# Gate bias of a two-layer graph network: VectorE adds it while moving the gate's product out of PSUM, in place of a matmul with rows of ones

## Reference

```python
h = jnp.maximum(_layernorm(x), 0.0)
hW = jnp.einsum('bnd,ade->bane', h, W)             # values of 12 heads of 32
th = jnp.tanh(hW)                                  # feeds the attention scores
attn = softmax(mask(leaky_relu(th @ w_src + (th @ w_dst).T)))
feat_out = elu(attn @ hW + b)
gate = jax.nn.sigmoid(h @ H_w.T + H_b)             # H_b is the gate's bias, 384 long
x = x + gate * feat_out + (1.0 - gate) * h
```

## Time and profile before

| | |
|---|---|
| median of 3 runs | 1082.45 us (1082.07 to 1084.26) |
| the profiled execution | 1083.79 us, of which the span from the first to the last instruction is 1082.0 us |
| mean granted TensorE clock | 0.979 |
| busy: TensorE matmul / weight loads | 993.6 us (92%) / 857.3 us (79%) |
| busy: VectorE, ScalarE, GpSimd | 770.1 us (71%), 574.4 us (53%), 273.5 us (25%) |
| matmuls of the bias (L665) | 64 |

### The profile page before, as it was taken

How to read it: one execution, slowest core, us unless ns; L and a number is a source line. 1 busy time by engine, 2 the same in 40 slices (tenths; PEclk the granted TensorE clock), 3 DMA queues, 4 the chain that set the end, 5 groups by cost and what they waited for, 6 DMA issues and landing times.

```text
span 1082.0 us, 24884 instructions
## 1 busy us (share of the span) xinstructions
PE 993.6 (92%) x10153; PEld 857.3 (79%) x10153; DVE 770.1 (71%) x1456; ACT 574.4 (53%) x1126; POOL 273.5 (25%) x338
## 2 busy tenths in 40 slices
PE   3779999999999999999999999999999999999686
PEld 3578888878788887878888787888878788887675
DVE  6576767788676768867677886767778677776814
ACT  5457456463844646375464637547364754735331
POOL 4023050421405032140503214050331405022120
PEclk9879999999999999999999999999999999999988
DMA  9202151330415122051411414151131414112102
GB/s 234 32 2 30 32 90 31 72 41 9 89 32 90 31 67 38 17 90 32 89 31 60 41 22 89 31 90 31 53 42 27 90 31 90 32 32 28 31 30 59
DMA packets 183654, 56.42 MB, mean 52 GB/s; under 512 B 164979, under 2 KB 183541, under 8 KB 183541
## 3 DMA queue, kind: packets, MB, share of 16 engines
q1 hardware_dynamic: 183540, 54.83, 28.4%
HBM read 17.06 MB, written 12.58 MB: 27 GB/s over the span
## 4 chain that ended last, share of the span: by engine, by line
PE 56%; DVE 28%; issue 7%; ACT 7%; SPq 1%; DMA 0%; POOL 0%; ACTq 0%; DVEq 0%; POOLq 0%
PE ps L620 11%; PE ps L622 10%; PE ps L621 10%; PE ps L606 10%; PE ps L688 5%; DVE x L935 4%; DVE ee L932 4%; PE ps L783 3%; DVE p L913 3%; ACT p L426 3%; DVE hT0l L851 3%; DVE hT1l L1034 3%; DVE stats L835 2%; DVE x_in L983 2%; PE ps L750 2%
## 5 line engine op out<-in xcount | busy, mean ns | idle before, releaser
L406 POOL TENSOR_TENSOR x_in<-x_in,ee 128x384 f32<-128x384 f32 x64 | 69.2, 1082 | 633.1 <-DVE ee L938 633.1
L465 ACT ACTIVATE th<-ps 128x384 f32<-128x384 f32 x64 | 31.9, 499 | 206.5 <-DVE v_tok L923 206.5
L971 DVE COPY_PREDICATED_SCALAR z<-not_adj,masked 128x768 f32 x64 | 69.3, 1084 | 32.1 <-ACT z L497 32.1
L606 PE MATMUL ps<-ident,p 128*128 128x128 f32 x576 | 75.8, 282 | 17.4 <-ACT p L426 10.0
L620 PE MATMUL ps<-Wf_hi,hT1h 128*128 128x384 f32 x192 | 70.5, 367 | 16.2 <-DVE hT1l L1034 10.4
L399 POOL TENSOR_TENSOR x_in<-x_in,h 128x384 f32<-128x384 f32 x64 | 84.6, 1352 | 0.1
L606 PEld LDWEIGHTS ps<-ident,p 128*128 128x128 f32 x576 | 65.9, 144 | 20.2 <-issue 12.6
L998 DVE TENSOR_TENSOR hT1l<-ps,hT1h 128x512 fp32r<-128x512 f32 x48 | 30.4, 684 | 67.3 <-ACT hT1h L536 67.2
L620 PE MATMUL ps<-W_hi,hT0h 128*128 128x384 f32 x192 | 65.9, 343 | 11.4 <-DVE b_plus L876 8.3
L395 POOL TENSOR_TENSOR x_in<-x_in,bf_row 128x384 f32<-128x384 f32 x64 | 62.4, 1009 | 48.1 <-ACT p L426 48.1
L503 ACT ACTIVATE z<-z 128x768 f32<-128x768 f32 x64 | 54.5, 853 | 28.1 <-DVE z L976 28.0
(11 more groups left out here) (130 smaller groups left out, 2825.7 us busy)
## 6 DMA issues: line engine op xcount, KB each, us to landing
V<-v_tok SPq DMA_DIRECT2D x128, 192.0 KB, 5.0
x_in<-in_x_dram SPq DMA_DIRECT2D x16, 768.0 KB, 5.0
out_dram<-x_in SPq DMA_DIRECT2D x16, 768.0 KB, 3.6
x<-in_L_gnn_H_w_dram SPq DMA_DIRECT2D x1, 576.0 KB, 5.9
QT<-in_L_gnn_W_dram SPq DMA_DIRECT2D x3, 192.0 KB, 6.7
thT<-in_L_gnn_Wq_dram SPq DMA_DIRECT2D x1, 576.0 KB, 6.1
z<-in_L_gnn_Wk_dram SPq DMA_DIRECT2D x1, 576.0 KB, 7.2
z<-in_L_gnn_Wv_dram SPq DMA_DIRECT2D x1, 576.0 KB, 8.2
```

The costliest lines, as they stand in the source:

```text
L406: pool.tensor_tensor(x_in[:, i % 3, t], x_in[:, i % 3, t], ee[:, t], ALU.subtract).then_inc(x2_made, 1)
L606: return pe.transpose(dst, src, ident[0:rows, 0:rows])
L971: dve.copy_predicated(zt, not_adj[:, t].unsqueeze(1).broadcast_to((P, HEADS0, N)), masked0[:].unsqueeze(2).broadcast_to((P, HEADS0, N))).t ...
```

## The change

The bias is no longer a matmul. The gate's product is 9 matmuls, and VectorE adds a full `H_b` row (held on all 128 partitions) while it moves the bank to `gate`; ScalarE's tanh then works on `gate` in place, in SBUF, and waits for VectorE. The gate's banks are released by VectorE's read. VectorE's new instructions stand between the `values0` calls. At the start the pieces that made the rows of ones and the split bias are gone, and one DMA that writes `H_b` to 128 partitions stands in place of the two small ones.

```diff
-        hb_rows = sb("hb_rows", [P, D], F32R)
-        ones_rows = sb("ones_rows", [P, P], F32R)
+        hb_row = sb("hb_row", [P, D])
...
-        pairs_of_jobs = zip(jobs("th_made", 0, th_made, 4), jobs("gate_tanh", 0, gate_tanh, 4))
+        pairs_of_jobs = zip(jobs("th_made", 0, th_made, 4), jobs("gate_biased", 0, gate_biased, 4))
...
-            sp.dma_start(x1[0:1, 3, :], H_b.rearrange("(a e) -> a e", a=1)).then_inc(consts_loaded, 16)
-            sp.dma_start(x1[32:33, 3, :], H_b.rearrange("(a e) -> a e", a=1)).then_inc(consts_loaded, 16)
+            sp.dma_start(hb_row[:], H_b.rearrange("(a e) -> a e", a=1).broadcast_to((P, D))).then_inc(consts_loaded, 16)
...
-            pool.memset(hb_rows[:].bitcast(F32), 0.0).then_inc(consts_made, 1)
...
-            for r in (0, 32):
-                act.activation(hb_rows[r:r + 1, :], x1[r:r + 1, 3, :], ACT.Copy).then_inc(rows_made, 1)
-            act.activation(ones_rows[:], ident[:], ACT.Identity, scale=0.0, bias=1.0).then_inc(rows_made, 1)
...
-                        act.wait_ge(gate_full, TILES * i + t + 1)
-                        if real(j):
-                            act.wait_ge(gated, TILES * j + t + 1)
-                        act.activation(gate[:, t], ps[:, job("gate_tanh", t) % BANKS, 0:D], ACT.Tanh, scale=0.5).then_inc(gate_tanh, 1)
+                        act.wait_ge(gate_biased, TILES * i + t + 1)
+                        act.activation(gate[:, t], gate[:, t], ACT.Tanh, scale=0.5).then_inc(gate_tanh, 1)
...
-                                lambda c: wh["Hw"][:, c], lambda c: wl["Hw"][:, c], more=True)
-                        pe.matmul(dst, ones_rows[:], hb_rows[:], start=False, stop=True).then_inc(gate_full, 1)
+                                lambda c: wh["Hw"][:, c], lambda c: wl["Hw"][:, c]).then_inc(gate_full, 1)
...
-            dve.wait_ge(rows_made, 2)
-            dve.tensor_tensor(hb_rows[32:33, :], x1[32:33, 3, :], hb_rows[32:33, :].bitcast(F32), ALU.subtract)\
-                .then_inc(small_ready, 1)
...
+                def gate_bias(t):
+                    if real(i):
+                        dve.wait_ge(gate_full, TILES * i + t + 1)
+                        dve.tensor_tensor(gate[:, t], ps[:, job("gate_biased", t) % BANKS, 0:D], hb_row[:], ALU.add).then_inc(gate_biased, 1)
...
                 values0(0)
+                gate_bias(0)
                 values0(1)
+                gate_bias(1)
                 if real(i):
...
                 values0(2)
+                gate_bias(2)
                 values0(3)
+                gate_bias(3)
```

More of the change, by code:

```diff
@@ L121, in two_layer_gnn @@
         ones_made = sem("ones_made")
-        rows_made = sem("rows_made")
+        gate_biased = sem("gate_biased")
         w_loaded = {k: sem(f"{k}_loaded") for k in ("W0", "Wq", "Wk", "Wv", "Wf")}
@@ L363, in _ @@
                                    pattern=[[-1, P]], channel_multiplier=1).then_inc(consts_made, 1)
-            pool.wait_ge(consts_made, 8)
+            pool.wait_ge(consts_made, 7)
             def inv_std(layer, g):
@@ L445, in _ @@
             h0_parts(0)
-            act.wait_ge(consts_loaded, 16 * 9)
-            act.wait_ge(consts_made, 8)
-            for r in (0, 32):
-                act.activation(hb_rows[r:r + 1, :], x1[r:r + 1, 3, :], ACT.Copy).then_inc(rows_made, 1)
-            act.activation(ones_rows[:], ident[:], ACT.Identity, scale=0.0, bias=1.0).then_inc(rows_made, 1)
+            act.wait_ge(consts_loaded, 16 * 8)
+            act.wait_ge(consts_made, 7)
             for name in w_late:
@@ L623, in product @@
                 return mm
-            pe.wait_ge(consts_made, 8)
+            pe.wait_ge(consts_made, 7)
             pe.wait_ge(hw_loaded, 16)
@@ L646, in _ @@
             turn_h0(NEXT, 0, 0)
-            pe.wait_ge(small_ready, 5)
-            pe.wait_ge(rows_made, 3)
+            pe.wait_ge(small_ready, 4)
             pe.wait_ge(w0_low, C)
@@ L660, in body @@
                                 lambda c: wh["W0"][:, c], lambda c: wl["W0"][:, c]).then_inc(values0_full, 1)
-                        take(i, job("gate_tanh", t))
-                        dst = ps[:, job("gate_tanh", t) % BANKS, 0:D]
+                        take(i, job("gate_biased", t))
+                        dst = ps[:, job("gate_biased", t) % BANKS, 0:D]
                         product(dst, lambda c: hT0h[:, c, toks], lambda c: hT0l[:, c, toks],
-                                lambda c: wh["Hw"][:, c], lambda c: wl["Hw"][:, c], more=True)
-                        pe.matmul(dst, ones_rows[:], hb_rows[:], start=False, stop=True).then_inc(gate_full, 1)
+                                lambda c: wh["Hw"][:, c], lambda c: wl["Hw"][:, c]).then_inc(gate_full, 1)
                 if real(i):
@@ L864, in _ @@
             h0_lows(0)
-            dve.wait_ge(consts_loaded, 16 * 9)
-            dve.wait_ge(consts_made, 8)
-            dve.wait_ge(rows_made, 2)
-            dve.tensor_tensor(hb_rows[32:33, :], x1[32:33, 3, :], hb_rows[32:33, :].bitcast(F32), ALU.subtract)\
-                .then_inc(small_ready, 1)
+            dve.wait_ge(consts_loaded, 16 * 8)
+            dve.wait_ge(consts_made, 7)
             for k, col in ((0, wcol), (HEADS0, wcol2)):
@@ L882, in _ @@
                                       ALU.subtract).then_inc(w_low, 1)
-            dve.wait_ge(small_ready, 5)
+            dve.wait_ge(small_ready, 4)
             heads_of = ident[:].rearrange("p (t r) -> p t r", r=SD)[:, :, 0:2 * HEADS0].rearrange("p t (s h) -> p t s h", h=HEADS0)
```

## The result

The changed kernel takes 1087.15 us (median of 6 runs, 1086.8 to 1087.4) against 1082.84 us (6 runs, 1082.0 to 1084.26): a ratio of 1.0038, 95% interval 1.0025 to 1.0051, so 4.3 us or 0.4% slower. The profiled execution took 1086.8 us with a span of 1085.0 us; TensorE's matmuls are busy 984.1 us (9.5 us less) and VectorE 800.9 us (30.8 us more).

The account below looks back on a forecast made before the run. ScalarE's last tanh of th, awaited by TensorE in 14 rounds, was taken as the bound; +5.2 us there and -1.0 us at the start and rounds 0 and 1 put 1082.45 at 1086.6 us, range 1083.2 to 1089.2.

Parts of the forecast that it names:

- What bounds the kernel: At the turn of th in rounds 2 to 15, TensorE waits 0.38 us each for ScalarE's last tanh.
- The removed matmuls: 64 bias matmuls, 0.69 us a round, 11.1 us in all; in rounds 2 to 15 they only lengthen TensorE's wait.
- VectorE paces ScalarE: Before normalise1, ScalarE's th and gate tanh slow from 0.375 to VectorE's 0.465 us pitch: +0.27 us; chance 0.66.
- The extra SBUF price: ScalarE's gate tanh reading SBUF costs 0.045 us more each; gate(0) hides it, gate(1) and gate(2) do not.
- The steady rounds: Rounds 2 to 15: th(3) comes later, so each round grows by 0.37 us, +5.2 us over 14 rounds.
- Start and rounds 0 and 1: Start 0.58 us earlier; round 0 gains 0.78 us including that, round 1 gains 0.2 us: together -1.0 us.
- Sum: Whole kernel: +5.2 - 1.0 = +4.2 us on the median 1082.45 us, giving 1086.6 us, +0.39%.
- B: At the start of a round ScalarE is hardly held by VectorE: 1083.4 us, chance 0.18.
- C: The saved matmuls come through because TensorE's products set when th is turned: about 1070.7 us, chance 0.08.
- D: TensorE's longer idle time at the turn of th lowers the granted clock: +38 us, 1124 us, chance 0.04.
- E: VectorE does not overlap its four alternating instructions, 0.585 us each instead of 0.465: 1091.9 us, chance 0.04.

Follow-up runs that it names:

- both doubled kernels: Changed kernel with the bias addition done twice, for tiles 0 and 1 (1104.28 us) or for tiles 2 and 3 (1090.48 us).
- The fastest version: Changed kernel, gates' tanh moved back, th(0) to th(2) ahead of normalise1 on ScalarE, values0(0) to values0(2) ahead of gate_bias on VectorE: 1068.42 us.

## Why the prediction held

**What bounds the kernel: right.** At the turn of `th` ScalarE is the last to arrive in rounds 2 to 15. Taking the matmuls out of the kernel before left its round as it was, and putting one back in the kernel after did too.

**The removed matmuls: right.** 0.69 us a round turned into wait. The wait went from 0.38 to 1.37 us; 1.44 was forecast. TensorE's busy time fell by 9.5 us where about 11 were forecast; I did not follow up the difference.

**VectorE paces ScalarE: right.** The pitch of 0.465 us is there. Doubling the addition on the path costs 0.92 us a round, off the path nothing. `normalise1` starts 2.41 us behind `values0(0)`; 2.4 was forecast. The extra SBUF price is right too: for three SBUF sources 0.135 us was forecast, and `th(3)` starts 0.13 us later with three.

**The steady rounds: +0.34 us against +0.37.** `th(3)` starts exactly 0.37 us later, but its tanh takes 0.47 us instead of 0.52 and so ends 0.32 later. I did not forecast that duration. It is 0.48 us too in the kernel in which nothing but the source of the gate's tanh was changed, so it comes with that source and not with VectorE; by what means, no run tells. This is the term that was too large: 14 x 0.34 = 4.8 us instead of 5.2.

**Start and rounds 0 and 1: -1.2 us against -1.0.** `values0(0)` of round 0 comes 1.0 us earlier (28.27 against 29.28) and not 0.58: besides the removed instruction the copies behind it now overlap with the one in front, some 0.1 us came from an earlier load, and a wait of 0.24 us fell away. Rounds 0 and 1 gain 0.07 and 0.11 us instead of 0.20 each; they are also the rounds where the clock varies (below). TensorE's first product starts at 21.96 where 22.2 was forecast (22.76 before).

**Sum: +4.2 us forecast, +4.3 us measured; that they agree to 0.1 us is luck.** The two terms were both off to the same side, and as measured they give 4.8 - 1.2 = +3.6 us. The profiled pair differs by 3.0 us in span: 1.0 and 0.2 us less up to the end of round 1, 4.7 us more in rounds 2 to 14, and 0.5 us less from the last `values0(0)` to the end (113.90 us after and 114.36 before), where the new round alone would add 0.3; the granted clock is 0.74 there against 0.66 in 20 us of it. The medians of the kernel before move by as much as this: 1082.84 in its first 6 runs, 1083.52 and 1084.08 in 17 and 23 later ones, which would make the changed kernel's 1087.15 us +3.6 and +3.1 us. So the totals support a slowdown of some 3 to 4 us, and the mechanism rests on the rounds.

**Rivals.** B is out: ScalarE is held fully. C is out by the two kernels that move the matmul alone. D did not happen in the changed kernel, where TensorE waits 1.37 us at each turn of `th` and the granted clock is 1.00 from 75 to 1029 us, that is until behind that wait of round 15. With 0.9 us more of waiting it did, at 1.5 to 2.5 us for a round it hits (2.7 was forecast) and not in every round. E is out: VectorE overlaps.

**Open.** Rounds 3 and 5 of the changed kernel are 0.20 and 0.26 us longer than the rest (63.97 and 64.03 us), and round 2 of the kernel before 0.15 us. The granted clock is 1.00 in all three, so it is not the clock. Two different delays show, in rounds 3 and 5:

```profile
248.45 0.47 PE L791 MATMUL ps<-V,KT 64*64 64x65 f32 x17 [0.69 <-issue]
...
339.92 1.09 ACT L522 ACTIVATE thT<-ps 128x512 f32<-128x512 f32 x2 [0.34 <-PE ps L598]
```

In round 3, as in round 2 of the kernel before (0.67 us), TensorE stops among the attention products and the profile shows nothing that it waits for. In round 5 the first copy of the turned `th` starts 0.27 us later in the round than elsewhere, although the transposes do not; it does so in round 5 of the kernel with the tenth matmul and of both doubled kernels too. What is behind either, no run tells.

## What to carry over

Moving an addition from the busiest engine to a less busy one pays only if the busy engine is the one that others wait for at that place: look at who waits at the next meeting point, and price the new hop there. Here VectorE's new instruction could run while ScalarE worked, and each hop cost the difference of the two pitches, 0.09 us, and not the instruction's 0.55 us; a second addition in the same place, with no work of ScalarE's to cover it, cost VectorE's whole pitch, 0.46 us. And ask what a move makes possible: here VectorE's read frees the PSUM banks early, so the tanh of the gate can leave the path, and with that reordering the kernel is 1.4% faster than before.

The reordering does not do this without the saved matmul. With the bias matmul in place TensorE could turn `th` only 0.38 us earlier, and the kernel before with the gates later does just that: it turns `th` directly behind the bias matmul. The fastest version's round is 0.94 us shorter. So more than half of its gain a round needs the 0.69 us that TensorE no longer computes, which were worth nothing as long as ScalarE came last. This is worked out from the rows; no run puts a tenth matmul into the reordered kernel.

## What the runs showed of the hardware

The first matmuls of round 1 follow an idle stretch, and their clock differs between kernels that do nearly the same work up to there (the one with the tanh from SBUF has one more memset at its start). The kernel before ran 69 to 75 us at 0.52; the one with the tanh from SBUF did the stretch at full clock:

```profile
69.00:75.00 6.00, 6.00 (x36) 6.00 (x36) 5.79 (x10) 0.00 (x0) 2.54 (x2) 1.00 0.01 3
```

36 matmuls against 20 in the same 6 us; its round 1 took 63.53 us and not 65.66. The idle time in front was the same in both, 3.08 and 3.09 us. Many runs of the kernel before, all unchanged, gather near 1082.1 us (mean clock 0.983) and near 1084.2 us (0.979 to 0.981). Others lie between or above. That distance is the size of this one stretch, but the end of the kernel is a rival of the same size: from the last `values0(0)` to the end the changed kernel took 113.90 us, and the one with tiles 2 and 3 doubled, with the same steady round, 116.09. I have not profiled both kinds, so the cause stays open; an effect under 2 us is better read from the length of the steady rounds than from medians.
